# Second attention: a second, turned score product in place of the transposes of the probabilities

## What is computed

```
xn   = layernorm(x)                                  # x: 8 x 512 x 512
q    = (xn @ w_q.T).reshape(8, 512, 16, 32)
k, v = ctx @ w_k.T, ctx @ w_v.T                      # ctx: 8 x 120 x 512
attn = softmax(einsum("bqhd,bkhd->bhqk", q, k) * 32 ** -0.5, axis=-1)
x    = x + einsum("bhqk,bkhd->bqhd", attn, v).reshape(8, 512, 512) @ w_o.T
```

## Time and profile before

| | us |
|---|---|
| time, median of 3 runs | 1243.57 |
| lowest and highest run | 1242.38 and 1247.81 |
| span of the profiled execution | 1257.6 |
| `attention1` alone on the engines, about | 250 to 600 of the span |

### The profile page before, as it was taken

How to read it: one execution, slowest core, us unless ns; L and a number is a source line. 1 busy time by engine, 2 the same in 40 slices (tenths; PEclk the granted TensorE clock), 3 DMA queues, 4 the chain that set the end, 5 groups by cost and what they waited for, 6 DMA issues and landing times.

```text
span 1257.6 us, 29419 instructions
## 1 busy us (share of the span) xinstructions
PE 1189.3 (95%) x10692; PEld 822.8 (65%) x10692; DVE 950.4 (76%) x2006; ACT 708.7 (56%) x1988; POOL 589.7 (47%) x685
## 2 busy tenths in 40 slices
PE   6888998799999999999999999999999998799996
PEld 3555665588888888786444445777777776466663
DVE  5889898899999999896677777777777775445460
ACT  4377788799899999896344322222222231365552
POOL 0047668737666667733200000445544345466744
PEclk9999999999999999999999999999999999899999
DMA  9522033134445454643870141221314320799987
GB/s 346 210 60 76 1 32 46 43 111 142 165 135 169 159 172 148 181 157 119 153 196 1 41 127 34 68 44 60 69 34 108 96 68 2 220 254 242 256 139 96
DMA packets 157567, 150.28 MB, mean 119 GB/s; under 512 B 78544, under 2 KB 111472, under 8 KB 157424
## 3 DMA queue, kind: packets, MB, share of 16 engines
q1 hardware_dynamic: 139584, 125.94, 35.5%
q0 software_dynamic: 13248, 21.15, 8.9%
q10 hardware_dynamic: 4592, 1.32, 0.6%
HBM read 84.93 MB, written 57.19 MB: 113 GB/s over the span
## 4 chain that ended last, share of the span: by engine, by line
PE 59%; DMA 17%; issue 8%; DVE 8%; POOL 5%; ACT 3%; ACTq 0%; SPq 0%; POOLq 0%; DVEq 0%
PE bank L121 28%; DMA lists<-att_land 14%; PE bank L1503 6%; PE bank L2125 5%; PE bank L955 4%; POOL lists L1629 4%; PE bank L1435 4%; PE bank L1456 3%; PE bank L1450 2%; PE bank L1421 2%; DMA q_rows<-att_land 1%; PE bank L1024 1%; ACT att_land L1353 1%; PE bank L872 1%; PE bank L891 1%
## 5 line engine op out<-in xcount | busy, mean ns | idle before, releaser
L1629 POOL DMA_INDIRECT lists<-att_land x128 | 134.4, 1050 | 310.7 <-DVE att_land L1770 166.8
L1353 ACT ACTIVATE att_land<-bank,att_land 128x120 f32<-128x120 f32 x512 | 178.3, 375 | 11.3 <-DVE att_land L1221 11.2
L2125 PE MATMUL bank<-att_land 128*128 128x512 f16 x768 | 177.3, 381 | 0.6 <-DVE program_logits L1304 0.6
L1952 ACT ACTIVATE att_land<-program_x 128x512 f32<-128x512 f32 x40 | 25.2, 631 | 195.2 <-DVE program_x L2094 165.1
L2125 PEld LDWEIGHTS bank<-att_land 128*128 128x128 f16 x768 | 75.4, 98 | 82.9 <-issue 2.0
L121 PE MATMUL bank<-program_xs,program_wgu 128*128 128x512 f16 x576 | 128.7, 379 | 0.6 <-DVE att_land L1729 0.6
L1353 ACT ACTIVATION_READ_ACCUMULATOR att_land<-bank,att_land 128x1 f32 x512 | 112.8, 221 | 0.0
L121 PE MATMUL bank<-att_land 128*128 128x128 f16 (+1 forms) x1560 | 101.0, 221 | 0.5 <-DVE att_land L1278 0.5
L121 PEld LDWEIGHTS bank<-program_xs,program_wgu 128*128 128x128 f16 x576 | 56.2, 98 | 67.5 <-DVE att_land L1729 1.1
L1221 DVE TENSOR_REDUCE att_land<-bank 128x4 f32<-128x480 f32 x128 | 82.4, 644 | 20.5 <-PE bank L1421 20.1
L1503 PE MATMUL bank<-att_land 128*128 128x512 f16 x384 | 93.4, 379 | 0.0
(11 more groups left out here) (305 smaller groups left out, 2817.2 us busy)
## 6 DMA issues: line engine op xcount, KB each, us to landing
att_land<-q_rows SPq DMA_DIRECT2D x96, 128.0 KB, 2.6
xn_rows<-att_land SPq DMA_DIRECT2D x37, 256.0 KB, 3.7
out_rows<-att_land SPq DMA_DIRECT2D x37, 256.0 KB, 6.4
q_rows<-att_land SPq DMA_DIRECT2D x32, 256.0 KB, 2.9
xt_tiles<-att_land SPq DMA_DIRECT2D x32, 256.0 KB, 2.1
x_rows<-program_x SPq DMA_DIRECT2D x8, 1024.0 KB, 4.8
att_land<-x_rows SPq DMA_DIRECT2D x8, 1024.0 KB, 5.6
program_xs<-xt_tiles SPq DMA_DIRECT2D x28, 256.0 KB
```

The source lines that it names most:

```text
L1353: last = act.activation(prob[:, c, h, :], ps_s[c % 2][:, h, :], ACT.Exp, bias=nmax[:, u % 2, c, h:h + 1], accum_out=rsum[:, u % 2, n:n + 1])
L1629: pool.indirect_dma_start(out=io["lists"], out_offset=bass.IndirectOffsetOnAxis(ap=index[:, t, k:k + 1], axis=0), in_=load[:, t, k, :], in ...
L2125: last = pe.matmul(ps_y[i][:, :], hid[:, c % 2, a, i * P:(i + 1) * P], wd[:, q, c, :], start=c == 0 and n == 0, stop=c == NC - 1 and n == 2)
```

## The change

The order of scores and transposes is replaced. `scores` now serves the maxima alone, in one bank, one chunk after the other. When a tile's 64 maxima columns (16 heads, one each) are known, PE turns them into 16 rows (`maxima_transposed`), DVE scales them by 1/64 and writes a float16 high and low part (`maxima_out`, two instructions, the second waits for the first), and SP issues two transfers of 16 x 128 float16 that lay them as rows 96 and 97 under the packed queries. The packed keys get two constant rows of 64 (`constant_rows`) and 32 zero columns. A second product (`scores_below`, 16 a tile, 98 rows, 128 x 128) gives the turned scores less their maxima. ACT takes the exponential of a whole chunk twice: once in float32 (`prob`), once in float16 (`pT` high). The low part moves from DVE to POOL. The values' high half gets a 33rd column of ones for each head, so that `outputs` gives the row sums too, in two banks; `inverse_sums` and `weighted` become two instructions each.

Also moved: the layernorms' application from POOL to ACT (`query_rows`, `gate_rows`, one pass with a scale and a bias; POOL makes the bias, one small instruction more), the weights' high half to ACT and low half to DVE. The packed queries have three places instead of two. The order within a step is new on every engine, two entries of `JOIN` move, and `shared` waits for `t_mm` (all turned scores) where it waited for `s_mm`.

```diff
-    spread(sp, g.keys[:, b % 2], io["k_rows"][b], (0, 1, 0), g.keys_in[b % 2])
+    spread(sp, g.keys[:, b % 2, :, 0:KC * J], io["k_rows"][b], (0, 1, 0), g.keys_in[b % 2])
...
-    spread(sp, g.queries[:, u % 2], io["q_rows"][u], (0, 0, 1), done[u % 2])
+    spread(sp, g.queries[u % 3], io["q_rows"][u], (0, 0, 1), done[u % 2])
...
+        pool.wait_ge(self.root, 2 * u + 1)
+        pool.tensor_scalar(self.shift[:, d], self.mv[:, d, 0:1], self.rstd[:, d], -1.0, ALU.mult,
+                           ALU.mult).then_inc(self.root, 1)
+    def scaled(self, act, g, u, d):
+        act.wait_ge(self.root, 2 * u + 2)
+        act.activation(self.xn[:, u % 2], g.x[:, u, :], ACT.Identity, scale=self.rstd[:, d],
+                       bias=self.shift[:, d]).then_inc(self.ok, 1)
...
-    prob = g.early(7 * D, [P, 4, HC, J])
+    prob = g.early(7 * D, [P, 3, HC, P])
+    nmax = g.early(SM, [P, 2, HC, KC])
+    below = g.early(SM + 2 * HEADS, [P, 2, 2, P], f16)
...
-    ps_sf, ps_p = (banks[1], banks[2]), chunked[3:5]
-    ps_s = [v[:, 0:HC * J].rearrange("p (h j) -> p h j", h=HC) for v in ps_sf]
+    ps_s = banks[1][:, 0:HC * J].rearrange("p (h j) -> p h j", h=HC)
+    ps_m = banks[1][0:HEADS, 0:P]
+    ps_t = chunked[2:4]
+    ps_o = [b[:, 0:HALF * (DH + 1)].rearrange("p (h o) -> p h o", h=HALF) for b in (banks[5], banks[4])]
...
                 sp.wait_ge(q_out[u % 2], 16 * (u // 2 + 1))
-                need(sp, c4["s_mm"], KC * (u - 1))
-                if u == 0:
+                need(sp, c4["t_mm"], KC * (u - 2))
+                if u == 2:
                     sp.wait_ge(f.a["sim"], NT)
                 packed_queries(sp, g, io, u, q_in)
+            if live(t):
+                sp.wait_ge(s["max_out"], 2 * t + 2)
+                for part in range(2):
+                    row = g.queries[t % 3][3 * DH + part:3 * DH + part + 1, :, :]
+                    sp.dma_start(row.rearrange("o r (c i) -> o (r c) i", i=P), below[0:HEADS, t % 2, part, :]) \
+                        .then_inc(max_in[t % 2], 16)
...
     def gpsimd(pool):
-        def apply(norm, mean, u):
...
+        def prob_low(u, c):
+            if live(u):
+                n = KC * u + c
+                pool.wait_ge(c4["exp"], n + 1)
+                pool.tensor_tensor(pT[0:J, c, 1], prob[0:J, n % 3], pT[0:J, c, 0], ALU.subtract).then_inc(c4["p_lo"], 1)
         def step(t):
             u = t - 4
             if live(u):
                 lg.inverse_root(pool, g, u, u % 4)
-                need(pool, rows_out[u % 2], 16 * (u // 2))
-                need(pool, s["g_tr"], u - 1)
-                apply(lg, s["mean_g"], u)
             yield
+            prob_low(t - 1, 0)
             u = t + 4
             if live(u):
                 ln.inverse_root(pool, g, u, u % 4)
-            u = t + 3
-            if live(u) and u >= HEAD:
...
-            if 3 < t <= 3 * B + 1 and t % 3 == 1:
-                b = t // 3 - 1
...
+            prob_low(t - 1, 1)
+            prob_low(t - 1, 2)
+            prob_low(t - 1, 3)
...
+            dve.tensor_reduce(nmax[:, u % 2, :, c], ps_s[:, :, :], AX.X, ALU.max, negate=True).then_inc(c4["max"], 1)
+        def maxima_out(u):
+            if live(u):
+                dve.wait_ge(s["max_tr"], u + 1)
+                need(dve, max_in[u % 2], 32 * (u // 2))
+                dve.tensor_scalar(below[0:HEADS, u % 2, 0], ps_m, 1 / STEP, None, ALU.mult).then_inc(s["max_out"], 1)
+                dve.wait_ge(s["max_out"], 2 * u + 1)
+                dve.scalar_tensor_tensor(below[0:HEADS, u % 2, 1], ps_m, 1 / STEP, below[0:HEADS, u % 2, 0], ALU.mult,
+                                         ALU.subtract).then_inc(s["max_out"], 1)
+        def constant_rows(slot):
+            if slot == 0:
+                dve.wait_ge(f.j_lo, f.jobs)
+            else:
+                dve.wait_ge(f.a["exp"], NT)
+            dve.memset(g.keys[3 * DH:3 * DH + 2, slot, :, :], STEP).then_inc(fixed, 1)
+            dve.memset(g.keys[0:3 * DH, slot, :, KC * J:4 * P], 0.0).then_inc(fixed, 1)
...
-                dve.wait_ge(c4["exp"], KC * u + KC)
-                need(dve, s["of"], u - 1)
-                dve.reciprocal(rinv[:, u % 2, :], rsum[:, u % 2, :]).then_inc(s["inv"], 1)
+                dve.wait_ge(c4["o_mm"], KC * u + KC)
+                for n in range(2):
+                    dve.reciprocal(rinv[:, u % 2, n * HALF:(n + 1) * HALF], ps_o[n][:, :, DH]).then_inc(s["inv"], 1)
         def weighted(u):
             if live(u):
-                dve.wait_ge(c4["o_mm"], KC * u + KC)
-                dve.wait_ge(s["inv"], u + 1)
+                dve.wait_ge(s["inv"], 2 * u + 2)
...
+                rows = of[:, :].rearrange("p (h o) -> p h o", h=HEADS)
+                for n in range(2):
+                    hs = slice(n * HALF, (n + 1) * HALF)
+                    last = dve.tensor_tensor(rows[:, hs, :], ps_o[n][:, :, 0:DH],
+                                             rinv[:, u % 2, hs].rearrange("p (h o) -> p h o", o=1).to_broadcast([P, HALF, DH]),
+                                             ALU.mult)
+                last.then_inc(s["of"], 1)
...
+        def weight_low(b):
+            dve.wait_ge(w_hi, b + 1)
+            dve.scalar_tensor_tensor(g.wgu[:, b, 1, :], raw[:, :], WS, g.wgu[:, b, 0, :], ALU.mult,
+                                     ALU.subtract).then_inc(w_lo, 1)
         def step(t):
-            maximum(t - 1, 3)
-            prob_low(t - 1, 0)
             query_low(t + 1)
+            maximum(t, 0)
+            inverse_sums(t - 2)
+            weighted(t - 2)
             rows_low(t + 2)
             yield
-            prob_low(t - 1, 1)
-            maximum(t, 0)
-            weighted(t - 2)
+            maximum(t, 1)
             logits(t - 5)
-            maximum(t, 1)
-            prob_low(t - 1, 2)
-            residual(t - 3)
-            gate_stats(t - 3)
-            maximum(t, 2)
-            aggregate(ln, t + 5)
             stats(ln, t + 6)
             first_rows(t + 3)
-            prob_low(t - 1, 3)
+            maximum(t, 2)
+            residual(t - 3)
+            maximum(t, 3)
+            gate_stats(t - 3)
+            maxima_out(t)
+            aggregate(lg, t - 3)
             output_low(t - 2)
-            aggregate(lg, t - 3)
+            aggregate(ln, t + 5)
             gate_low(t - 4)
-            inverse_sums(t - 1)
+            if 3 < t <= 3 * B + 1 and t % 3 == 1:
+                weight_low(t // 3 - 1)
+            if t in (-1, 1):
+                constant_rows((t + 1) // 2)
...
     def scalar(act):
-        def prob_high(u, c):
+        def exps(u, c):
             if not live(u):
                 return
-            act.wait_ge(c4["p_mm"], KC * u + c + 1)
-            need(act, c4["o_mm"], KC * (u - 1) + PLACE[c] + 1)
...
-            pe.wait_ge(c4["exp"], KC * u + c + 1)
-            need(pe, c4["p_lo"], KC * u + c - 1)
-            for h in range(HC):
-                last = pe.transpose(ps_p[c % 2][0:J, h, :], prob[:, c, h, :], g.ident[:, :])
-            last.then_inc(c4["p_mm"], 1)
-        def outputs(u, c):
-            if not live(u):
-                return
-            if c == PLACE.index(0):
+            if c == 0:
                 need(pe, s["of"], u)
...
             pe.wait_ge(c4["p_lo"], KC * u + c + 1)
             for h in range(HC):
-                cols = slice((c * HC + h) * DH, (c * HC + h + 1) * DH)
-                for n, (a, b) in enumerate(((0, 0), (0, 1), (1, 0))):
-                    last = pe.matmul(ps_o[:, cols], pT[0:J, c, a, h, :], g.v1[0:J, b, u // TB, cols],
-                                     start=n == 0, stop=n == 2)
+                head = c * HC + h
+                out = ps_o[head // HALF][:, head % HALF]
+                pe.matmul(out, pT[0:J, c, 0, h, :], g.v1_high[0:J, u // TB, head, :], start=True, stop=False)
+                pe.matmul(out[:, 0:DH], pT[0:J, c, 0, h, :], g.v1_low[0:J, u // TB, head, :], start=False, stop=False)
+                last = pe.matmul(out, pT[0:J, c, 1, h, :], g.v1_high[0:J, u // TB, head, :], start=False, stop=True)
             last.then_inc(c4["o_mm"], 1)
...
         def step(t):
-            outputs(t - 2, 0)
-            outputs(t - 2, 2)
-            prob_transposed(t - 1, 0)
-            scores(t - 1, 3)
+            scores(t, 0)
             outputs(t - 2, 3)
             rows_transposed(t + 2)
-            prob_transposed(t - 1, 1)
-            scores(t, 0)
+            scores_below(t - 1, 0)
+            product(t - 3, 0)
+            scores(t, 1)
+            scores_below(t - 1, 1)
             yield
-            product(t - 3, 0)
-            prob_transposed(t - 1, 2)
             gate_logits(t - 5)
+            product(t - 3, 1)
+            scores(t, 2)
+            outputs(t - 1, 0)
+            output_transposed(t - 2)
+            scores_below(t - 1, 2)
+            scores(t, 3)
             queries(t + 2, 0)
-            scores(t, 1)
-            product(t - 3, 1)
-            prob_transposed(t - 1, 3)
```

(18 more changed lines are left out.)

230 lines of the change are left out of this document (115 added, 115 removed).

## The result

The prediction was wrong: 1272.36 us (median of 4 runs, 1271.29 to 1277.1) against 1244.14 (median of 4) for the kernel before, measured beside it. The ratio is 1.0226, 95% interval 1.0196 to 1.0256, so the change costs 2.3%, 28 us, where a gain of 11 was forecast and 1250 was the upper end of the range. (The text on the change has a slip: a tile's maxima are 16 columns, 4 heads in each of 4 chunks, not 64.)

What follows compares the result with a forecast made beforehand. PE's own work was taken to bound `attention1`. The terms -26.7 + 5.8 + 4.5 + 2.4 + 3 = -11.0 us, from the median 1243.57, gave 1232.6; forecast 1225 to 1241, 8-in-10 range 1216 to 1250.

Steps and rivals of the forecast that it cites:

- PE's work: PE's own work in a step of `attention1`: 9.92 us against 10.84 before, 26.7 us gained over 29 steps.
- three signs of being wrong: PE's slots differ, the maxima's transfer lands after more than 2.65 us, or `front`'s end moves by more than 7.
- the maxima's transfers: Round trip between a tile's two products: 3.6 us with a landing of 2.3, covered by PE's 3.76, no stall.
- the first rival: Last chunk and query rows arrive in time, so the stalls vanish: -21 us, 1218 with a quiet start; chance 0.15.
- Start and end: Overlap with `front`, memsets and the first tile's maxima: 3 us lost at the start; nothing at the end.
- two trips of the maxima: Upper bound of the loss at the start: two round trips of 3.6 us each.
- the last chunk: At the step's end `outputs` 3 wait for POOL's low part: 0.2 us a step, 5.8 in all.
- the weights: Weights' low part at the end of DVE's step delays the next one: eight times 0.3, 2.4 us.
- the rival built on it: Last chunk gives the gain back: ACT and POOL 0.4 later, stall 0.6, time 1244; chance 0.15.
- Late query rows: Query rows land late where keys, weights and rows fall together: 1.5 us three times, 4.5; bounds 0 and 12.
- The drain: The last tiles, after which `shared` begins: changes at the end were left at nothing.
- 29 counted steps: Steps of `attention1` credited with 0.92 us each, since the first three fill beside `front`.

Runs made afterwards that it cites:

- e5: Changed kernel with the edits of e3 and e4 together; ratio 1.0165 to the kernel before.
- e8: e5 with SP's big transfers put behind the query rows, finished rows stored tile by tile; ratio 1.0112 to the kernel before.
- e9: e12 plus two score banks for tiles 0 and 1 and the query products of steps 0 and 1 between their scores; ratio 0.9998.
- e12: Changed kernel with the edits of e4, e3, e6, e8 and e1, finished rows behind the gate rows' store, weights loaded in halves in two steps; ratio 1.0015.
- e14: e13 with the second attention's steps from 1 on behind `front`'s last; 1242.30 us, ratio 0.9980 to the kernel before.
- e11: Changed kernel without the maxima's transfers, maxima left out of the turned scores, exponentials of a 64th of the scores; ratio 1.0218.
- e10: Changed kernel with the scores of tile 0 alone alternating between two banks; ratio 1.0182 to the kernel before.
- e6: e4 with the constant rows' memsets moved from VectorE to POOL, the second two steps later; ratio 1.0141.
- e4: Changed kernel with `rows_low` put ahead of the reciprocals and weighted outputs on VectorE; ratio 1.0132 to the kernel before.
- e3: Changed kernel with the last chunk's low part moved from POOL to VectorE, ahead of `gate_low`; ratio 1.0199 to the kernel before.
- e13: Changed kernel with all steady fixes, its own join with `front`, constant rows on POOL and two score banks for tile 0; ratio 1.0000.
- e1: Changed kernel with all second-attention steps from 0 on put behind `front`'s last step on each engine; ratio 1.0144.

## Why the prediction was wrong, point by point

**PE's work was right.** 9.92 was forecast, and 9.94 is the step wherever nothing waits (e5, e8, e9, e12 to e14). Outputs with 33 columns cost nothing extra. Of the three signs of being wrong that the prediction named, two did not come: PE's slots are as forecast, and the maxima's transfers landed after 1.8 and 2.2 us (median; 2.3 was taken, 2.65 was the limit). The third did: `front`'s end moved by 15 us, and 7 was the limit. That the landing came out near 2.3 is in part luck: the prediction says that no transfer of so few bytes is in the trace, but two of 2 KB are, on another engine's queue, and they landed later:

```profile
att_land<-in_L_bq ACTq DMA_DIRECT2D x1, 2.0 KB, 3.5
att_land<-in_L_bk ACTq DMA_DIRECT2D x1, 2.0 KB, 4.9
```

(A sum of the first rival is also off by 1: with a quiet start it gives 1219, not 1218.)

**The step that failed first is "Start and end".** It was given 3 us, between 0 and two trips of the maxima (7.2); it was 20.9, and e11 shows that the trips had no part in it. The start was priced by the new thing that travels. What cost was a thing taken away: the second bank of the scores, which had let PE go one burst ahead of VectorE while `front`'s work lay between. e10 shows 8.6 of it; the memsets, mentioned and not priced, are 4.5 (e6); `rows_low` first gave 2.0 (e4; 1.8 from e3 to e5) and step 1 behind `front` 1.9 (e13 to e14). These are 17.0 one by one and 16.2 together in e14; 4.7 stay open. The change part by part listed "in one bank" and drew no wait from it, because in a full step there is none. PE's lower clock after such waits (0.86 and 0.80 over these 100 us) stretches each of these; in the kernel before it was 1.00 in this stretch, and it was in no bound.

**The second is the order on VectorE at the turn of the step.** Its load was found lower by 1.3 us, which is about right, and "what counts is when results arrive" was then worked out for the last chunk and the weights alone. For `rows_low`, which stands behind the reciprocals and the weighted outputs, nobody was named as waiting; the logits do, by way of a shared bank. Alone this chain sets 10.44 in a quiet step (e3), and 11.37 in the weights' steps. Over 25 steps the quiet 10.44 against 9.94 is 12.5; the weights' 0.93 in eight steps is 7.4, where 2.4 was forecast, and e4 brings it to 0.3 a step, the price I had given it.

**The last chunk on POOL** was sized well: 0.2 forecast, 0.26 measured. But it lay beside the longer chain to the logits, so that taking it away alone gave nothing (e3), and 0.3 once that chain was shorter (e4 to e5). POOL's pass is 1.16 against 0.69 for the same pass on VectorE in e3, 1.7 times. The Trainium skill, GPSIMD Engine Reference, section Engine selection, says about twice as slow for two operands; the rows stay below it, and the rival built on it (1244) was not the cause.

**Late query rows** were sized about right. Three of the five long steps wait for them (1.5, 1.6 and 1.7 us); above 10.44 these take 5.4 us, where 4.5 in three steps was forecast. 3.0 of it is the longest, 13.45, in which PE's granted clock stood at 0.89 from 490 to 506: I had counted the wait and not the slow PE behind it. The other two (11.31 and 13.35, together 3.8 above 10.44) have waits of 0.9 and 0.8 for the maxima's transfers, which were given no stall, and one of 0.8 for a maximum.

**The drain** was left at nothing and is 6.2 us longer. There PE waits for POOL's low parts (3.2 us from 560 to 650) and for maxima (1.5), with little else to do. e1 has the same code there and the same waits, 3.2 and 1.5, but its last six tiles take 58.5 us instead of 61.5: its granted clock stays at 1.00, where the changed kernel's fell to 0.83 from 590 to 600 and to 0.85 from 610 to 620. So about half of the 6.2 are the lower clock of this execution, and 3.2 remain without it. Without the last low part on POOL and with the transfers moved it is 57.6 or 57.7 (e8, e13, e14); e9 and e12 have 60.7, with a granted clock of 0.91 from 560 to 600.

**The sum again.** Start 20.9 instead of 3. Steps: 25 x 10.44 = 261.0, and 7.4 and 9.1 make 277.5 (277.6 measured), where the terms as forecast (9.92, 0.20 for the last chunk, 0.24 for weights and query rows) would have given 259. Drain 6.2 longer, where the four of the 29 counted steps that lie in it would have made it 1.9 shorter. The gain on PE of 0.9 a step was real, and waits of other engines' work took it; e14, in which most of the losses are undone, has a mean step of 10.38 and shows 0.45 of it. That this is close to the 10.36 of the forecast is in part luck: its weights' steps take 0.7 more than a quiet one, not 0.3, and the 0.20 for the last chunk is not in it.

## What to carry to other kernels

Taking away a buffer can cost where the two engines are not in step: look at the pipeline's fill, and ask for each wait there what of the neighbouring stage is queued behind it on both engines. When PE's work in a step shrinks, list every consumer on PE with the instruction that it waits for and that instruction's new place in its engine's order, shared banks included; of two waits in a row the one on the longer chain hides the other, so judge the second only with the first taken away. A transfer that was just in time can be late once the step is shorter: put the loads that the next step needs first ahead of the bulky ones.
